# A linear-attention and expert block: the values' product with two heads stacked on 128 contraction rows

## The reference, cut to what matters

```python
q, k = silu(x @ Wq), silu(x @ Wk); v = x @ Wv        # 16 heads of 8
q, k = [q cos, q sin], [k cos, k sin]                 # 16 wide per head
mask = tril(ones(n, n))
energy = einsum('bhnd,bhmd->bhnm', q, k) * mask
out    = einsum('bhnm,bhmd->bhnd', energy, v)
x = layernorm(x + layernorm(out @ Wo * sigmoid(x @ G1 @ G2)))
```

## Time and profile before

| | us |
|---|---|
| median of 3 runs (lowest, highest) | 820.63 (820.49, 820.79) |
| span of the profiled execution, first to last instruction | 819.0 |
| mean granted TensorE clock over the span | 0.988 |
| PE busy (PEld) | 771.5 (627.2) |
| DVE busy | 583.9 |
| ACT busy | 368.2 |
| POOL busy | 415.7 |
| DMA queues of SP and of POOL, share of 16 engines | 23.2%, 11.0% |

### The profile page before, as it was taken

The page is one execution under the profiler, slowest core; times in us unless marked ns, Lnnn a source line. Parts: engine busy times, 40 slices in busy tenths (PEclk is TensorE's granted clock), DMA queues, the critical chain, the costliest instruction groups (busy, mean ns, idle before and its releaser), DMA issues.

```text
span 819.0 us, 30731 instructions
## 1 busy us (share of the span) xinstructions
PE 771.5 (94%) x12462; PEld 627.2 (77%) x12462; DVE 583.9 (71%) x1865; ACT 368.2 (45%) x802; POOL 415.7 (51%) x395
## 2 busy tenths in 40 slices
PE   5889999999999999999998889899999999999994
PEld 4667777777777777778776677688999989899884
DVE  7488798888888888898868898845444454544674
ACT  6334564646546465564633332223322333323484
POOL 6441243523435243342534555671677778876442
PEclk9999999999999999999999999999999999999997
DMA  4155233231333323233322212114444455433455
GB/s 148 46 174 180 78 92 85 64 93 53 100 76 78 90 57 97 61 86 77 77 64 54 69 34 70 42 53 137 98 87 58 80 98 102 72 52 42 126 151 145
DMA packets 71163, 70.56 MB, mean 86 GB/s; under 512 B 11443, under 2 KB 54250, under 8 KB 71024
## 3 DMA queue, kind: packets, MB, share of 16 engines
q1 hardware_dynamic: 53928, 52.33, 23.2%
q0 software_dynamic: 17024, 16.28, 11.0%
q10 hardware_dynamic: 72, 0.00, 0.0%
HBM read 23.99 MB, written 28.89 MB: 65 GB/s over the span
## 4 chain that ended last, share of the span: by engine, by line
PE 78%; DVE 10%; issue 4%; DMA 3%; SPq 2%; POOL 2%; ACT 1%; POOLq 0%; DVEq 0%; ACTq 0%
PE energy_banks L1935 5%; PE bank L1853 5%; PE energy_and_gate_banks L1853 5%; PE bank L1855 5%; PE bank L1854 5%; PE energy_and_gate_banks L2409 4%; PE bank L2409 4%; PE energy_and_gate_banks L1960 4%; PE energy_and_gate_banks L1855 3%; PE energy_and_gate_banks L1854 3%; PE bank L1894 3%; PE energy_banks L1853 3%; PE energy_banks L1855 3%; PE energy_banks L1854 3%; PE bank L1895 2%
## 5 line engine op out<-in xcount | busy, mean ns | idle before, releaser
L626 POOL DMA_INDIRECT dispatched_rows<-x,slot x128 | 140.0, 1093 | 224.5 <-PE energy_banks L1935 132.4
L760 POOL DMA_INDIRECT summed_rows<-VP,goal_i x80 | 123.8, 1548 | 42.5 <-issue 22.7
L1119 ACT ACTIVATE sq<-energy_banks 128x512 f32<-128x512 f32 (+1 forms) x96 | 50.5, 526 | 120.2 <-PE energy_banks L1855 118.5
L842 ACT ACTIVATE hidden_rounded<-sf 128x512 fp32r<-128x512 f32 x88 | 55.3, 628 | 58.8 <-DVE sf L1273 58.0
L832 ACT ACTIVATE sf<-energy_and_gate_banks 128x512 f32<-128x512 f32 x88 | 52.4, 596 | 62.2 <-PE energy_and_gate_banks L1855 60.8
L1273 DVE TENSOR_TENSOR sf<-sf,bank 128x512 f32<-128x512 f32 x88 | 60.1, 683 | 19.4 <-PE bank L1855 19.2
L1935 PE MATMUL energy_banks<-EM,VP 64*32 64x64 f32 x4096 | 59.1, 225 | 1.1 <-issue 1.1
L1243 DVE TENSOR_TENSOR EM<-energy_and_gate_banks,causal 128x512 f32<-128x512 f32 x64 | 43.9, 686 | 18.7 <-PE energy_banks L1960 18.7
L1853 PE MATMUL energy_and_gate_banks<-xgT_hi,ws_hi 128*128 128x512 f32 x108 | 52.1, 482 | 3.4 <-DVE EM L1243 2.6
L1935 PEld LDWEIGHTS energy_banks<-EM,VP 64*32 64x32 f32 x4096 | 47.8, 105 | 4.2 <-issue 3.2
L1853 PE MATMUL bank<-xgT_hi,ws_hi 128*128 128x512 f32 x108 | 45.9, 425 | 3.7 <-DVE sf L1273 1.4
(11 more groups left out here) (255 smaller groups left out, 2178.4 us busy)
## 6 DMA issues: line engine op xcount, KB each, us to landing
QM<-QT SPq DMA_DIRECT2D x248, 32.0 KB
dispatched_rows<-empty POOLq DMA_DIRECT2D x8, 655.0 KB
QM<-dispatched_rows SPq DMA_DIRECT2D x8, 655.0 KB, 6.2
QT<-sq SPq DMA_DIRECT2D x40, 128.0 KB
KT<-sq SPq DMA_DIRECT2D x40, 128.0 KB
xin<-in_x SPq DMA_DIRECT2D x16, 256.0 KB, 2.9
QM<-summed_rows SPq DMA_DIRECT2D x16, 256.0 KB, 2.8
out_x<-QM SPq DMA_DIRECT2D x16, 256.0 KB, 3.2
```

The source lines that it names most:

```text
L626: g.indirect_dma_start(out=xg_d, out_offset=bass.IndirectOffsetOnAxis(ap=slot[:, n % 2, j:j + 1], axis=0), in_=x1[:, n % 2, j % NC, :], in ...
L760: g.indirect_dma_start(out=sum_d, out_offset=bass.IndirectOffsetOnAxis(ap=goal_i[:, par, t:t + 1], axis=0), in_=ye[:, par, t, :], in_offse ...
L842: a.activation(hs_hi[:, f], sf[:, n % SF], ACT.Copy).then_inc(a_hh, 1)
```

## The change

- **attend**: one product now contracts 128 rows: 64 keys of one head and, below them, 64 keys of another. For each half s and pair there is one product of 128 rows by 32 columns: 16 products, 32 PE instructions per call. It waits for a new semaphore, `vp_in` >= 32 (b + 1).
- **energies**: the loops are put in the order s, t2, r; the energies of the two heads of a pair must stand on different partitions, so row group r writes output rows 64 ((r + t2) mod 2) of bank t2 of `EG2` (r = 0, 1) or `EB2` (r = 2, 3). Two row groups now write to one bank, on different partitions.
- **values** puts a half's values with one 128x256 copy contiguously into `VN`; *state* reads them there.
- **pair_values** (new, POOL, L627 to L634 of the changed kernel): three copies on 128 partitions (256, 128 and 128 elements) put the heads' values that stay on their partitions into the new `VP`, at the start of step b (in the opening for block 0, behind its eight q_by_head).
- **stage_values** (new, ACT): three copies on 64 partitions (256, 128 and 128 elements) put the others in the same layout into `VS`.
- **move_values** (new, SP, L431 to L436): two DMAs of 256 KB each take `VS` to the other 64 partitions of `VP`. They wait for both of the above and stand at the start of step b ahead of `xin`, for block 0 in the opening between SP's two groups of q_by_head.
- In the opening: one more clear on ACT, Wv's columns swapped by group (two copies each on ACT and POOL in place of one).

```diff
+            def move_values(b, par):
+                need(sp, a_vs, 3 * (b + 1))
+                need(sp, g_vp, 3 * (b + 1))
+                sp.dma_start(VP[T:P, par, 0], VS[0:T]).then_inc(vp_in, 16)
+                sp.dma_start(VP[0:T, par, 1], VS[T:P]).then_inc(vp_in, 16)
             def step(b, par):
+                if 0 < b < B:
+                    move_values(b, par)
...
+            def pair_values(b, par):
+                need(gp, a_v, 4 * b + 4)
+                need(gp, pe_av, 4 * (b - 1))
+                need(gp, z_vp, min(b, 1) + 1)
+                g.tensor_copy(by_pair(VP[:, par, 0], slice(0, P), 0), heads(par, slice(0, P), 0)).then_inc(g_vp, 1)
+                for t2 in (0, 1):
+                    g.tensor_copy(by_pair(VP[:, par, 1], slice(0, P), 1, t2), heads(par, slice(0, P), 1, t2)).then_inc(g_vp, 1)
...
-                for c in (0, 1):
-                    src = PB[i][:, 256 * c:256 * c + D].rearrange("p (j i d) -> p j i d", j=4, i=4)
-                    a.activation(vp_view(par, 2 * i + c), src, ACT.Copy).then_inc(a_v, 1)
+                a.activation(VN[:, par, 2 * i:2 * i + 2], PB[i][:].rearrange("p (c n) -> p c n", c=2)[:, :, 0:D], ACT.Copy).then_inc(a_v, 2)
...
+            def stage_values(b, par):
+                need(act, a_v, 4 * b + 4)
+                need(act, vp_in, 32 * b)
...
             def attend(b, par, c):
                 need(pe, pe_sm, 4 * b + c + 1)
+                need(pe, vp_in, 32 * (b + 1))
-                for i in range(4):
+                for g in (0, 1):
                     for s in (0, 1):
-                        keys = slice(T * s, T * (s + 1))
-                        for j in range(4):
-                            h = 4 * j + i
-                            ins = t.matmul(AV2[32 * j:32 * j + 32, s, cols], VP[keys, par, c, 32 * h:32 * h + 32],
-                                           EM[keys, c % 2, h % 8 // 4, h % 4 // 2 * 4 + h // 8 * 2 + h % 2],
+                        for j in (0, 1):
+                            for t2 in (0, 1):
+                                o, pair = T * t2 + 32 * j, 32 * (4 * j + 2 * t2 + g)
+                                ins = t.matmul(AV2[o:o + 32, s, cols], VP[:, par, s, c, pair:pair + 32], EM[:, c % 2, j, 4 * t2 + 2 * s + g],
...
             def energies(c):
-                    for t2 in (0, 1):
-                        for s in (0, 1):
+                    for s in (0, 1):
+                        for t2 in (0, 1):
                             for r in range(4):
-                                ins = t.matmul((EG2, EB2)[r // 2][T * s:T * (s + 1), r % 2, 2 * T * t2:2 * T * (t2 + 1)],
+                                rows, o = slice(32 * r, 32 * r + 32), T * ((r + t2) % 2)
+                                ins = t.matmul((EG2, EB2)[r // 2][o:o + T, t2, 2 * T * s:2 * T * (s + 1)],
```

More of the change, by code:

```diff
@@ L115, in build @@
         Kt = sb("Kt", [P, 2, NC, 256])
-        VP = sb("VP", [P, 2, NC, 512])
+        VP = sb("VP", [P, 2, 2, NC, 256])
+        VN = q_space[:, 4 * S:6 * S].rearrange("p (b c n) -> p b c n", b=2, c=NC)
+        VS = q_space[:, 6 * S:8 * S].rearrange("p (c n) -> p c n", c=NC)
         EM = sb("EM", [P, 2, 2, 8, T])
@@ L326, in normed_before, with by_pair, heads, groups_swapped @@
             return min(max(b - 2, 0), DIRECT)
+        def by_pair(v, rows, upper, t2=None):
+            w = v[rows]
+            steps = [[40, 4]] if not upper else [[40, 2]]
+            return bass.AP(tensor=w.tensor, offset=w.offset + (16 + 48 * t2 if upper else 0), ap=[list(w.ap[0]), [128, 2 * NC], *steps, [1, 8]])
+        def heads(par, rows, upper, t2=None):
+            w = VN[rows, par]
+            steps = [[48, 2]] if not upper else []
+            return bass.AP(tensor=w.tensor, offset=w.offset + (16 + 16 * t2 if upper else 0), ap=[list(w.ap[0]), [64, 2 * NC], *steps, [1, 16]])
+        def groups_swapped(w):
+            return w[:, 0:D].rearrange("p (t j n) -> p j t n", t=2, j=2)
         def by_copy(w):
@@ L465, in step @@
                             q_by_head(sp, 1 - par, g2, h, g_qm[g2])
+                        if b == -1 and g2 == 0:
+                            move_values(0, 0)
                 if b == B:
@@ L632, in fill @@
                     gp.dma_start(xg_r[e], empty[:]).then_inc(g_fill, 16)
+                if b == -1:
+                    pair_values(0, 0)
+                elif 0 < b < B:
+                    pair_values(b, par)
                 if b in (1, 2):
@@ L786, in clear @@
                 return a.activation(t.rearrange("p (a n) -> p a n", n=P), zeros[:].unsqueeze(1).broadcast_to([P, count // P, P]), ACT.Copy)
-            clear(VP[:, 0].rearrange("p c n -> p (c n)"), 4 * 512).then_inc(z_vp, 1)
+            clear(VP[:, 0].rearrange("p s c n -> p (s c n)"), 4 * 512).then_inc(z_vp, 1)
             act.wait_ge(ld_q, 16)
@@ L903, in opening @@
                     act.wait_ge(a_g, 1)
-                    a.activation(wvg_hi, wvg_s, ACT.Copy).then_inc(a_wvg, 1)
+                    a.activation(wvg_hi[:, 0:D].rearrange("p (j t n) -> p j t n", j=2, t=2), groups_swapped(wvg_s), ACT.Copy).then_inc(a_wvg, 1)
+                    a.activation(wvg_hi[:, D:2 * D], wvg_s[:, D:2 * D], ACT.Copy).then_inc(a_wvg, 1)
+                    clear(q_space[:, 6 * S:8 * S], 2 * S).then_inc(z_vs, 1)
                     for i in range(4):
                         silu(f, fp, i)
-                    act.wait_ge(z_vp, 1)
                     values(f, fp, 0)
                     values(f, fp, 1)
+                    stage_values(f, fp)
                     input_hi(1)
@@ L917, in first_blocks @@
                     else:
-                        clear(VP[:, 1].rearrange("p c n -> p (c n)"), 4 * 512).then_inc(z_vp, 1)
+                        clear(VP[:, 1].rearrange("p s c n -> p (s c n)"), 4 * 512).then_inc(z_vp, 1)
                     if b > 0:
                         copy_out(b - 1, 3, 1 - par)
+                        stage_values(b, par)
                     silu(f, fp, 0)
@@ L2295, in v_rows @@
             def v_rows(par, c, half, j, tok):
-                v = VP[tok, par, c]
-                return bass.AP(tensor=v.tensor, offset=v.offset + 256 * half + 128 * j, ap=[list(v.ap[0]), [40, 4], [1, 8]])
+                return VN[tok, par, c, T * j + 32 * half:T * j + 32 * half + 32]
             stage1(pe, step)
```

28 lines of the change are left out of this document (18 added, 10 removed).

## The result

Slower: 843.5 us median of four runs (839.73 to 846.72) against 820.56 for the kernel before; the ratio is 1.0271, with a 95% interval of 1.0241 to 1.0302. The direction was the forecast one, the size was not: +22.9 us where +3.2 was expected, outside the range that ended at 831. The runs of the changed kernel differ by 7 us among themselves. The profiled one is the fastest of them, 838.0 us from its first to its last instruction, 19.0 more than before.

A forecast was written before the change was run, and what follows sets the result against it. PE's stream was taken to bound the kernel, busy 94% of the span. Terms 3.4 - 5.7 - 0.5 + 0.7 + 0.5 + 3.8 + 1.0 = +3.2 on 820.6 gave 823.8 us, range 816 to 831.

The forecast's parts named there:

- the values stand 3.4 us after the copies: Moves into VP: two DMAs, priced like xin's 2.9 us landing plus a second issue some 0.5 later; range 2.3 to 4.5.
- Opening to step 2: Uncovered waits at attend(0,0), (1,0) and (2,0), with shifts of SP's queue and QT's turn: together +3.4 us (1.5 to 6).
- ACT's staging runs beside POOL's and is no longer: Supply of the values: ACT's staging copies were taken to run alongside POOL's pair copies, adding no time.
- Clock: Stalls at attend(0,0), (1,0) and (15,0): half a further drop to 1.2 GHz, +1.0 us (0 to 4).
- Steps 12 to 15: Late steps of stage 1: -0.5 in step 12, +0.7 in 13, +0.5 in 14, +3.8 us in 15.
- Steps 3 to 11: Feed-forward steps: three of four attend calls each pass on a 0.21 us gain, nine steps, -5.7 us; supply hidden.
- Rival 2: A change of array shape on either side of attend, 0.10 us more per call: +2.9, 826.7 us; chance 0.08.
- Rivals 3: attend's rounds of four tiles take as long as rounds of eight, so no gain: 830.2 us; chance 0.09.
- 5 (energies take turns): Two row groups sharing a PSUM bank go one after the other, 0.42 us more per call: +27, 851 us; chance 0.04.
- 6 (half the time): attend's half as many products take half the time, -29.5 with the same waits: 800 us; chance 0.02.
- Rival 4: Copies 0.7 and landing 1.1 us longer at five waiting places: +9 less what idle time takes, 831 us; chance 0.10.
- Rival 1: Step 15's late PE stall lies beside DVE's backlog and is made up, without the clock cost: 817.1 us; chance 0.22.

The follow-up runs named there:

- run with the supply unread: Changed kernel, but pairing, staging and moves fill the tile's second half while attend reads the cleared first half without waiting; one clear less: 815.94 us, ratio 0.9957.
- run without supply: Changed kernel without pair_values, stage_values, move_values and the wait for them; attend reads a cleared tile: 816.37 us, ratio 0.9959.
- early supply: Changed kernel, ACT writing the values that stay; blocks 1, 2, 13 to 15 staged a step earlier, moved between SP's q_by_head groups: 822.72 us, ratio 1.0029.

## Why the prediction was wrong in size

Right: the bound (PE), the cost per round, the places of the waits (0, 1, 13, 14 and 15; block 2 waited too), the cover in the feed-forward steps (the moves were hidden there but for one wait of 0.3 us in block 9), the queue that stands ahead of each wait, and the sign.

**The step that failed is the price of the moves, "the values stand 3.4 us after the copies (2.3 to 4.5)".** It was taken from xin, an input from DRAM that lands alone after 2.9 us. Measured from the end of POOL's copies to attend: 5.2 us in block 0, 4.6 in 13 and 14, 5.4 in 15, all beyond the upper bound; in blocks 1 and 2, from the end of the sixteen q_by_head, 5.0 and 4.8. xin's own landing rose to a median of 4.0 beside the moves. Whether the moves are slow because two go together or because they go from partition to partition was not tested. At six waits this term alone is 1.2 to 2.0 us each, some 9 us added up; not all of it reaches the end, since the wait of block 13 was made up.

**"Opening to step 2: together +3.4"** measured +12.3. The run with the supply unread has attend(3,0) at 101.0, so 10.9 of the 12.3 hang on the waits and on what follows them. The chain was the forecast one, down to the turn of QT that no longer ran beside POOL's split of the weights (0.68 us at 54.20 instead of 2.15), but each of its links was longer: SP's sixteen q_by_head began 4.1 us late rather than with the first wait's 1.6, the moves behind them landed 4.4 after issue, and attend(2,0) waited 2.6 in its own right, where I had put that wait "inside" SP's shift. One term was put at nothing without a reason: "ACT's staging runs beside POOL's and is no longer" holds, but in the opening it stands ahead of the keys, and with the clock that fell behind it made attend(0,0) 2.0 us late before the moves were due.

**"Clock: +1.0 (0 to 4)"** was priced by the three drops seen before. There were eight stretches and 47.8 us in stage 1 instead of 10.2. By PE's busy time the price is some 11 us over the whole run. This is mixed with the early term, because most of the low stretches lie in steps 0 to 2, and the two were not separated further.

**"Steps 12 to 15"**: +4.5 forecast (-0.5, 0.7, 0.5, 3.8), +8.4 measured (-2.3, 0.2, 3.0, 7.5 by step). The wait of block 15 was 6.7 instead of 4.4. PE's wait of block 13 was made up (attend(13,1) is 5.4 late, as attend(12,3) had been 5.1), that of block 14 was not (8.1 and 8.4).

**"Steps 3 to 11: -5.7"** measured -4.9, and the mechanism held: a call gained 0.20 (0.21 forecast), and the gain of one call was lost at the gate's bank. That the 0.20 came out so close is partly luck. Rival 2 was right on the change of shape: attend of 128x32 pays on entry (0.09) and again on exit to 128x128, where 0.15 us lie between the last start and the next line's and a round takes 0.05. Against it, the calls before were longer on average than the one row that the prediction took.

Rivals 3 (no gain in attend), 5 (energies take turns) and 6 (half the time) fell by the trace: 0.59 against 0.79, 0.63 per call of the energies, 0.59 and not 0.4. Rival 4, transfers at their upper bound, 831 us, was nearest: its landing is what the runs bear out, and went past the bound, while the copies at the waits stayed below theirs; the clock's loss came on top. Rival 1 (the late stall is made up) fell: attend(15,0) is 14.9 late and attend(15,3) 15.8.

What stays open: how the clock and the waiting share the loss in the early steps; why the low stretches that begin ahead of a wait came; and the 7 us between runs of the same changed kernel, of which the profile shows the fastest, so that 3.9 of the 22.9 us are in no trace.

## What to carry to other kernels

When a layout that makes a matmul cheaper has to be built by other engines, price the chain that builds it first: here the product gained 0.2 us per call, and the chain of small copies, queue places and a landing left PE standing 1.2 to 6.7 us wherever no step's work covered it. The same chain cost nothing that could be measured when it started as soon as its inputs existed, on an engine that was idle there and in a queue with nothing ahead. Count rounds and tiles, not instructions: half as many products of four tiles are as many rounds as twice the number of eight.

## What the runs showed of the hardware

- Rounds of eight small tiles are slower than rounds of four: 64 products in eight tiles have 0.64 us from the first start to the last in the shortest call (0.77 in the longest seen), 32 in four tiles 0.435, for eight rounds each, 80 and 54 ns a round.
- Going from 64-row to 128x32 tiles costs 0.09 us, and going on from there to 128x128 costs again. The Trainium skill, "TensorEngine Tiling (Array Packing)", section "Key Properties", says that a change of tiling mode drains the engine; the trace agrees for both: 0.09 us on the way in, and on the way out 0.15 us from attend's last start to the next line's, where a round takes 0.05.
- Two row groups that write different partitions of one PSUM bank run side by side as fast as in two banks, 0.63 us per call of the energies against 0.62. The Trainium skill, same page, section "Restrictions and Gotchas", says that different row tiles cannot access the same bank simultaneously; here, on different partitions, they could, and the measurement decides.
- A DVE copy of 64x256 took 0.28 us alone and 2.97 beside POOL's adds; POOL's own pair copies of 128x256 took 0.39 to 0.41 us in the opening and in steps 2, 13 and 14, and 0.93 in the feed-forward steps.
- PE stood 2.05 us in the middle of one attend, between two products that no wait separates, put down to "issue", while the DMA engines were busy to 80% (window 66 to 72 us of the run without supply). The same call has such a gap in four other kernels, 0.4 us with the early supply and 1.8 to 2.9 in the rest. What it waited for no view shows, and no run was made to tell it.
